# Cross-attention and a ternary feed-forward block: one pass of the attention loop put in another order on four engines

## The chip, the core and the metric

The kernel runs on one core of a Trainium2 chip. The metric is device time in microseconds (us) of one execution. Before the change it is 221.17 us, the median of 3 runs (220.5 to 221.46).

## What is computed

Eight sequences of 256 tokens with 256 features, x, attend with 16 heads of 16 to a context of 64 keys each, and pass a feed-forward block of 1024 hidden units with ternary weights and quantised activations. Scores are masked causally, so only the keys up to a token's number count.

```python
x = x + xattn(layernorm(x), ctx, Wq, Wkv_expand, Wout)     # softmax(q k^T / 4, causal) v, then Wout
h = layernorm(x)
x = x + linear_bit(silu(linear_bit(h, w1, g1)) * linear_bit(h, w2, g2), w3, g3)

def linear_bit(x, w, g):
    xq = act_quant(g * x * rsqrt(mean(x * x) + 1e-8))      # rounds x * 127 / max|x| of each token
    s = mean(|w|); wq = round(tanh(w / (s + 1e-8))) * arctanh(s)
    return xq @ wq.T
```

## The kernel before, in words

Every engine's program is written out by hand, one function per step, and the order of the calls in each engine's block is the order in which it executes. Engines wait for each other through one semaphore per kind of step (`need(engine, semaphore, value)`).

**Attention** works on one batch (one sequence, two tiles of 128 tokens) at a time. Iteration j of the loops (`def iteration(j)` on GpSimd at L398, TensorE L618, ScalarE L806, VectorE L1055) holds the second half of batch j and the first half of batch j+1. The scores of both tiles fill the PSUM tensor `wide` (4 banks); bank4 to bank7 serve everything else. In the order of one batch's data: `scores` (TensorE L511, masks first at L500), `maximum` per token and head (VectorE L907), `split_maxima` into three bf16 parts (L913, L916), `maxima_T` (TensorE L520), `maxima_T_copy` (VectorE L922), `subtract_maxima` by a matmul onto the scores (L527), `exponentials` (ScalarE L765), `half_sums` of 32 and 32 keys (GpSimd L337), `sums` with the reciprocal (VectorE L926, L929), `recip_widen` (ScalarE L751), `recip_T` (TensorE L536, through the helper at L475) and `recip_T_copy` (ScalarE L757), `probs_T` (TensorE L547, L475) and `probs_T_copy` in four pieces (L745), `weigh` (L558), `divide` (VectorE L934), `project` (L580), `residual` (VectorE L940).

Into the same iterations other work is woven: the next queries in two halves (`query`, L492, copied by ScalarE at L735), the first layer norm's statistics and power (`measure`, `aggregate`, GpSimd `norm` L327, L329), and for the feed-forward input of batch j-1 its statistics (L945, L950), GpSimd's `factor` (L343 to L348), `centre_gain` into the tile u (L958), `token_max` (L965), GpSimd's `token_scales` (L352, L356), `token_recip` (L970), `token_quant_scales` (L361), ScalarE's `quantise` (L785), `tokens_T` (L564) and its copy (L791). The weights are made ternary on the way: absolute sums (L771), means (L989), `series` and `log_input` and `log_branch` for arctanh (L994 to L1016, three elements wide), tanh (L777), `ternary` (L974).

Before the loops TensorE warms up (`keep_warm`), folds the mean into Wq (L589), and computes keys (L595), queries (L492) and values (L483) from two copies of the context that are loaded side by side into one tile (L246).

**The feed-forward loop** runs over 16 tiles T of 128 tokens: `up` in two halves (L660), `silu` (L842), `gated` (VectorE L1095), `gained` by g3 (GpSimd L425, the last tile on VectorE L1100), `square` (ScalarE L848), `scales` (GpSimd L431 to L449), `hidden_max` (VectorE L1107), `hidden_scale` (L1113, L1116), `quantise_hidden` (ScalarE L854), `hidden_T` (L671) and its copy (VectorE L1122), `down` (L684), `finish` (L1129), store. Between the loops stand the rest of batch 7's attention, and batches 5 to 7's tokens; `column_sums` (L695, copied at L1135) is needed once, before the first `down`.

In the trace a matmul of float32 shows as two passes, so that 8 rows are 4 transposes.

## Time and profile before

| What | Value |
|---|---|
| median of 3 runs | 221.17 us |
| the profiled execution, whole | 221.68 us |
| its span, first to last instruction | 219.8 us |
| mean granted TensorE clock | 0.898 of full speed |
| busy: PE, DVE, ACT, POOL | 166.9, 154.8, 143.2, 122.5 us |
| HBM traffic | 9.04 MB read, 2.10 MB written |

PE is TensorE, DVE is VectorE, ACT is ScalarE, POOL is GpSimd. The granted clock is 1.00 at 2.4 GHz and 0.50 at 1.2 GHz; a value between them in a stretch is the mean of both levels. A profile says how long each instruction was on its engine, what released an engine that had been idle, and the chain of instructions and waits that ended last. Idle time counts only where something later hangs on it.

### The profile page before, as it was taken

How to read it: one execution, taken by the hardware profiler on the slowest of the kernel's cores; microseconds unless marked ns; L12 is line 12 of the kernel's file. 1: busy time of each engine (PE TensorE's matmuls, PEld its weight loads, DVE VectorE, ACT ScalarE, POOL GpSimd, SP SyncE). 2: the span in 40 equal slices, each digit the busy share in tenths (PEclk: the TensorE clock that was granted, in tenths of full speed). 3: DMA queues.
4: the chain of work that ended last, by engine and by line, in shares of the span. 5: the costliest groups of instructions: out<-in, count | busy, mean ns of one | idle time of the engine just before them, and what ended most of it. 6: DMA issues, size and time to landing. Idle time of an engine off the chain costs nothing.

```text
span 219.8 us, 3409 instructions
## 1 busy us (share of the span) xinstructions
PE 166.9 (76%) x1114; PEld 113.1 (51%) x1114; DVE 154.8 (70%) x297; ACT 143.2 (65%) x193; POOL 122.5 (56%) x230
## 2 busy tenths in 40 slices
PE   8699679794895796696593993896666998998543
PEld 7177556563763664554562663362334464645332
DVE  0328253984689785775894896089698999999982
ACT  2033557861763865855882968658979998989740
POOL 8142807137054237238256183327789999999950
PEclk9769799999589679679999797589999999999999
DMA  7999910000000000000000000000000010100102
GB/s 145 319 378 368 374 65 0 0 4 1 0 1 0 3 0 0 0 3 0 0 1 0 3 0 0 0 3 0 0 25 25 27 48 28 48 24 24 51 24 72
DMA packets 9216, 11.35 MB, mean 52 GB/s; under 512 B 1584, under 2 KB 7984, under 8 KB 9200
## 3 DMA queue, kind: packets, MB, share of 16 engines
q1 hardware_dynamic: 8656, 10.62, 14.6%
q10 hardware_dynamic: 544, 0.52, 1.3%
q8 instruction: 9, 0.15, 0.3%
q14 instruction: 7, 0.06, 0.1%
HBM read 9.04 MB, written 2.10 MB: 51 GB/s over the span
## 4 chain that ended last, share of the span: by engine, by line
issue 21%; PE 21%; POOL 19%; DVE 18%; ACT 17%; DMA 3%; SPq 1%; POOLq 0%; DVEq 0%; ACTq 0%
ACT q_x L785 6%; PE bank L475 6%; POOL half_sum L337 5%; PE bank L492 4%; DVE row_sum L926 3%; POOL w_in L425 3%; DMA ctxT<-in_ctxT 3%; DVE u L958 2%; ACT probsT L745 2%; PE wide L511 2%; ACT wT L771 2%; PE wide L595 2%; POOL m_h L435 2%; ACT recipT L757 2%; POOL fb_a L346 2%
## 5 line engine op out<-in xcount | busy, mean ns | idle before, releaser
L425 POOL TENSOR_TENSOR w_in<-hh,g3b 128x1024 f32<-128x1024 f32 x15 | 35.4, 2360 | 1.1 <-DVE hh L1095 1.1
L660 PE MATMUL wide<-wT,xqT 128*128 128x512 bf16 x128 | 31.4, 388 | 2.2 <-DVE hh L1095 2.2
L475 PE MATMUL bank<-ident,probs 128*128 128x128 f32 x128 | 23.0, 339 | 8.6 <-ACT probsT L745 8.6
L327 POOL TENSOR_SCALAR ln_ve<-ln_mv 128x2 f32<-128x2 f32 x8 | 1.8, 227 | 46.8 <-DVE ln_mv L894 46.8
L684 PE MATMUL bank<-wT,hT 128*128 128x256 bf16 x128 | 16.7, 274 | 10.9 <-DVE hT L1122 10.0
L475 PEld LDWEIGHTS bank<-ident,probs 128*128 128x128 f32 x128 | 19.0, 176 | 11.5 <-issue 11.2
L745 ACT COPY probsT<-bank 128x512 f32<-128x512 f32 x32 | 17.6, 587 | 9.7 <-PE bank L475 9.7
L854 ACT ACTIVATE q_h<-w_in,round_c,qs_h 128x1024 f32<-128x1024 f32 x16 | 19.9, 1241 | 5.9 <-DVE qs_h L1116 5.9
L765 ACT ACTIVATE probs<-wide,ln_rstd 128x1024 f32<-128x1024 f32 x16 | 17.0, 1112 | 8.8 <-PE wide L527 8.8
L337 POOL TENSOR_TENSOR half_sum<-probs 128x512 f32<-128x512 f32 x16 | 21.9, 1389 | 0.8 <-ACT probs L765 0.8
L926 DVE TENSOR_REDUCE row_sum<-half_sum 128x32 f32<-128x1024 f32 x8 | 9.7, 1218 | 17.7 <-POOL half_sum L337 17.7
L492 PE MATMUL bank<-xT,wqT 128*128 128x256 f32 x64 | 21.7, 478 | 0.0
L684 PEld LDWEIGHTS bank<-wT,hT 128*128 128x128 f16 x128 | 11.4, 98 | 18.4 <-DVE hT L1122 16.2
L848 ACT ACTIVATE sq_junk<-hh,root_x 128x1024 bf16<-128x1024 f32 x16 | 18.3, 1144 | 2.9 <-DVE hh L1095 2.9
L1095 DVE TENSOR_TENSOR hh<-w_in,wide 128x1024 f32<-128x1024 f32 x16 | 19.3, 1209 | 0.5 <-PE wide L660 0.5
L660 PEld LDWEIGHTS wide<-wT,xqT 128*128 128x128 bf16 x128 | 11.8, 99 | 15.0 <-DVE hh L1095 2.9
L1107 DVE TENSOR_REDUCE c_max<-w_in 128x1 f32<-128x1024 f32 x16 | 19.4, 1212 | 0.0
L907 DVE TENSOR_REDUCE max_part<-wide 128x16 f32<-128x1024 f32 x16 | 18.8, 1211 | 0.5 <-PE wide L511 0.5
L842 ACT ACTIVATE w_in<-wide,dq_x 128x1024 f32<-128x1024 f32 x16 | 17.7, 1104 | 2.3 <-PE wide L660 2.3
L475 PE MATMUL bank<-ident,recip_w 128*128 128x128 f32 x32 | 6.0, 317 | 17.0 <-ACT recip_w L751 17.0
L511 PE MATMUL wide<-k_diag,qT 64*128 64x256 f32 x128 | 17.0, 403 | 0.0
L492 PEld LDWEIGHTS bank<-xT,wqT 128*128 128x128 f32 x64 | 13.7, 234 | 6.2 <-issue 4.3
(138 smaller groups left out, 360.7 us busy)
## 6 DMA issues: line engine op xcount, KB each, us to landing
out<-y SPq DMA_DIRECT2D x16, 128.0 KB, 1.7
w_in<-in_w1T SPq DMA_DIRECT2D x1, 1024.0 KB, 7.9
w_in<-in_w2T SPq DMA_DIRECT2D x1, 1024.0 KB, 11.8
w_in<-in_w3T SPq DMA_DIRECT2D x1, 1024.0 KB, 13.0
xT<-in_xT SPq DMA_DIRECT2D x1, 1024.0 KB, 9.4
x_sb<-in_x SPq DMA_DIRECT2D x1, 1024.0 KB, 11.9
x_sb<-in_x SPq DMA_DIRECT2D x2, 256.0 KB, 5.7
xT<-in_xT SPq DMA_DIRECT2D x1, 512.0 KB, 8.7
```

The costliest lines, as they stand in the source:

```text
L337: last = g.tensor_tensor(out=half_sum[:, t, :, :], in0=e[:, :, 0, :], in1=e[:, :, 1, :], op=ALU.add)
L425: g.tensor_tensor(out=c_h[:, t, :], in0=hh[:, t, :], in1=g3b[:], op=ALU.mult).then_inc(c_ready, 1)
L475: return nc.tensor.matmul(out, in_, ident[0:n, 0:n], is_transpose=True, start=True, stop=True)
L492: last = nc.tensor.matmul(bank5[:, oc * S:(oc + 1) * S], wqT[:, kc, oc * P:(oc + 1) * P], xT[:, kc, b * S:(b + 1) * S], start=(kc == 0), s ...
L511: last = nc.tensor.matmul(wide[:, n:n + PR * SK], qT[rows, c, t * P:(t + 1) * P], k_diag[rows, b % 2, c, :, :], start=(t == 1 and c == 0), ...
L660: last = nc.tensor.matmul(wide[:, (w * 2 + n) * 512:(w * 2 + n + 1) * 512], xqT[:, T, w * DC + c, :], wT[:, cols:cols + 512], start=(c == ...
L684: nc.tensor.matmul(down_banks[t][:, 0:D], hT[:, t, n, :], w_cols[:, n, :], start=(n == 0), stop=False)
L745: a.copy(probsT[:, c * PR:(c + 1) * PR, t * P:(t + 1) * P], halves[c][:].rearrange("p (n s) -> p n s", s=P)).then_inc(pT_ready, 1)
L854: a.activation(q_h[:, t, :], c_h[:, t, :], ACT.Identity, scale=qs_h[:, t:t + 1], bias=round_c[:, 2:3]).then_inc(qh_ready, 1)
L907: v.tensor_reduce(out=max_part[:, 2 * t:2 * t + 2, 0, :], in_=by_head(wide, t).rearrange("p (g n) k -> p g n k", g=2), op=ALU.max, axis=AX ...
L1095: v.tensor_tensor(hh[:, t, :], gate[:, t, :], wide[:, H:2 * H], ALU.mult).then_inc(hh_ready, 1)
L1107: v.tensor_reduce(out=c_max[:, t:t + 1], in_=c_h[:, t, :], op=ALU.max, axis=AX.X, apply_absolute_value=True).then_inc(cm_ready, 1)
```

## The change

On TensorE the maxima's transpose goes to bank5 and the transposes of the reciprocals are called behind it, behind all of the probabilities' transposes; the subtraction is called before the query's first half. ScalarE copies the reciprocals' transposes after the probabilities'. GpSimd calls `values` and `factor` before, `norm` after the half sums. VectorE takes the statistics of batch j-1 before the maxima's copy, `centre_gain` before `measure`, `ternary` before `token_max`, and the three-element weight steps after `sums`; `log_branch` moves into the middle of iteration 6. The tile u is doubled. The context comes already doubled in its layout in memory and is loaded by one transfer; four warm-up matmuls are added. An activation of one element with Exp is added behind Ln. Between the loops and in the first eight tiles of the feed-forward loop steps of batches 5 to 7 are called at other tiles.

```diff
-        u = sb("u", [P, TB, 2, D])
+        u = sb("u", [P, 2, TB, 2, D])
...
-                for n in range(2):
-                    sp.dma_start(ctxT[:, :, n, :], ctxT_d.rearrange("l (b k) -> l b k", k=SK)).then_inc(ctx_ld, 16)
+                sp.dma_start(ctxT[:].rearrange("l b n k -> l (b n k)"), ctxT_d).then_inc(ctx_ld, 16)
...
                     if live(j + 2):
                         keys(j + 2)
-                        norm(j + 2)
                     if j >= 1:
-                        factor(j - 1)
-                    if j >= 1 and live(j + 1):
...
                         values(j + 1)
-                    if live(j + 1):
-                        half_sums(j + 1)
+                        factor(j - 1)
+                    if j == B - 2:
+                        pool.wait_ge(w_down_ready, 1)
+                        product_scales(0, 4)
+                    half_sums(j + 1)
+                    if live(j + 2):
+                        norm(j + 2)
                     if j >= 1:
                         token_scales(j - 1)
...
-                pool.wait_ge(w_down_ready, 1)
-                product_scales(0, 6)
+                product_scales(4, 2)
...
-                    if T == 0:
+                    if T == 1:
                         token_scales(6)
-                    if T == 1:
+                    if T == 2:
                         token_quant_scales(6)
                         product_scales(6, 1)
-                    if T == 2:
                         factor(7)
+                    if T == 4:
                         token_scales(7)
-                    if T == 3:
+                    if T == 5:
                         token_quant_scales(7)
                         product_scales(7, 1)
...
                 def maxima_T(b):
                     need(pe, parts_ready, b + 1)
-                    need(pe, rT_ready, b)
+                    need(pe, qT_ready, b + 1)
...
-                    nc.tensor.matmul((bank4 if b else bank6)[:].bitcast(bf16)[:, 0:P], top_half(parts), ident_h[:],
+                    nc.tensor.matmul((bank5 if b else bank6)[:].bitcast(bf16)[:, 0:P], top_half(parts), ident_h[:],
...
                     need(pe, rT_ready, b + 1)
-                    if live(b + 1):
-                        need(pe, maxT_ready, b + 2)
...
                 last.then_inc(mean_done, 1)
+                keep_warm(4)
                 pe.wait_ge(wkv_ld, 16)
-                pe.wait_ge(ctx_ld, 32)
+                pe.wait_ge(ctx_ld, 16)
...
-                for oc in range(DC):
-                    query(1, oc)
+                query(1, 0)
                 pe.wait_ge(sel_ready, 1)
                 maxima_T(0)
                 pe.wait_ge(v_early, 1)
                 values_of(4)
                 subtract_maxima(0)
+                query(1, 1)
...
                 def iteration(j):
+                    scores(j + 1)
                     if j == 0:
                         pe.wait_ge(v_late, 2)
-                    if live(j + 1):
-                        scores(j + 1)
-                    if j > 0:
-                        recip_T(j)
+                    if j == 2:
+
+                        pe.wait_ge(inv_ready, 1)
                     probs_T(j, 0)
                     probs_T(j, 1)
-                    if j == 0:
-                        recip_T(j)
                     maxima_T(j + 1)
+                    recip_T(j)
+                    subtract_maxima(j + 1)
                     if live(j + 2):
                         query(j + 2, 0)
-                    subtract_maxima(j + 1)
                     weigh(j)
...
+                recip_T(7)
                 up(1, 0)
-                recip_T(7)
                 weigh(7)
-                tokens_T(5)
-                project(7)
-                column_sums()
                 for T in range(NT + 2):
                     t = T % TB
                     if live_tile(T + 1):
                         up(T + 1, 1)
+                    if T == 0:
+                        project(7)
                     if live_tile(T + 2):
                         up(T + 2, 0)
+                    if T == 1:
+                        column_sums()
...
-                    if T == 2:
-                        need(pe, xqT_ready, 6)
-                        tokens_T(6)
+                    if T == 0:
+                        need(pe, pT_ready, 4 * B)
+                        tokens_T(5)
                     if T == 4:
                         need(pe, y_ready, 2)
+                        tokens_T(6)
+                    if T == 6:
+                        need(pe, y_ready, 4)
                         tokens_T(7)
...
+                abs_sums(1)
                 act.wait_ge(half_set, 1)
 
                 def iteration(j):
-                    if j > 0:
-                        recip_widen(j)
+                    recip_widen(j)
                     if j >= 2:
                         quantise(j - 2)
-                    if j > 0:
-                        recip_T_copy(j)
                     probs_T_copy(j, 0)
-                    if j == 0:
-                        recip_widen(j)
                     probs_T_copy(j, 1)
-                    if j == 0:
-                        recip_T_copy(j)
+                    recip_T_copy(j)
                     exponentials(j + 1)
...
+                        a.activation(warm_exp[:], round_c[:, 1:2], ACT.Exp)
...
+                    if j == 6:
+                        log_branch()
                     maximum(j + 1, 0)
                     maximum(j + 1, 1)
                     split_maxima(j + 1)
...
                         measure_sum(j - 1)
+                        aggregate_sum(j - 1)
                     maxima_T_copy(j + 1)
+                    if j >= 1:
+                        centre_gain(j - 1)
                     if live(j + 2):
                         measure(j + 2)
-                    if j >= 1:
-                        aggregate_sum(j - 1)
-                        centre_gain(j - 1)
-                    if live(j + 2):
                         aggregate(j + 2)
                     divide(j)
+                    if 3 <= j < 6:
+                        ternary(j - 3)
                     if j >= 1:
                         token_max(j - 1)
-                    if 3 <= j < 6:
-                        ternary(j - 3)
+                    sums(j + 1)
                     if j == 1:
                         weight_means()
                     if j == 2:
                         series()
+                    if j == 3:
                         log_input()
-                    if j == 6:
-                        log_branch()
-                    sums(j + 1)
...
-                residual(7)
-                column_sums_copy()
                 for T in range(NT + 3):
                     t = T % TB
                     if T > 0 and live_tile(T):
                         gated(T, t)
+                    if T == 1:
+                        residual(7)
+                        measure_sum(7)
```

`log_branch` needs Ln's result from iteration 5. On the host `ctxT` is now `np.repeat(ctx[:, None], 2, axis=1)` in that layout, and SK is worked out from its doubled length.

TensorE in iteration 4, from the end of the scores (L511, in the change L512) to the projection, before:

```order
L475 MATMUL bank<-ident,recip_w 128x128 x4
L475 MATMUL bank<-ident,probs 128x128 x16
L520 MATMUL bank<-ident_h,max_part 128x128
L492 MATMUL bank<-xT,wqT 128x256 x2
L527 MATMUL wide<-neg_sel,maxT 128x512 x4
L558 MATMUL bank<-probsT,v_pair 32x256 x8
L492 MATMUL bank<-xT,wqT 128x256 x2
L564 MATMUL bank<-ident_h,q_x 128x128 x8
L580 MATMUL bank<-woutT,attnT 128x256 x4
```

TensorE at the same place in the change:

```order
L476 MATMUL bank<-ident,probs 128x128 x16
L521 MATMUL bank<-ident_h,max_part 128x128
L476 MATMUL bank<-ident,recip_w 128x128 x4
L528 MATMUL wide<-neg_sel,maxT 128x512 x4
L493 MATMUL bank<-xT,wqT 128x256 x2
L557 MATMUL bank<-probsT,v_pair 32x256 x8
L493 MATMUL bank<-xT,wqT 128x256 x2
L563 MATMUL bank<-ident_h,q_x 128x128 x8
L579 MATMUL bank<-woutT,attnT 128x256 x4
```

The reciprocals' transposes (`recip_w`) went from the head of the pass to a place behind the maxima's, and the first half of the query (`xT,wqT`) from in front of the subtraction (`neg_sel`) to behind it.

GpSimd in iteration 4, from `token_quant_scales` to the half sums, before:

```order
L361 TENSOR_TENSOR qs_x<-rm_x,fb_127a 128x4
L312 TENSOR_TENSOR k_diag<-kT,head_in 128x512
L327 TENSOR_SCALAR ln_ve<-ln_mv 128x2
L329 TENSOR_TENSOR ln_rstd<-ln_ve,neg_half 128x2
L343 TENSOR_SCALAR fb_ve<-fb_mv 128x2
L346 TENSOR_TENSOR fb_a<-fb_ve,neg_half 128x2
L348 TENSOR_SCALAR fb_127a<-fb_a 128x2
L320 TENSOR_TENSOR v_pair<-v_all,key_half 128x256
L337 TENSOR_TENSOR half_sum<-probs 128x512 x2
```

GpSimd in the change, iteration 4, from `token_quant_scales` to `norm`:

```order
L361 TENSOR_TENSOR qs_x<-rm_x,fb_127a 128x4
L312 TENSOR_TENSOR k_diag<-kT,head_in 128x512
L320 TENSOR_TENSOR v_pair<-v_all,key_half 128x256
L343 TENSOR_SCALAR fb_ve<-fb_mv 128x2
L346 TENSOR_TENSOR fb_a<-fb_ve,neg_half 128x2
L348 TENSOR_SCALAR fb_127a<-fb_a 128x2
L337 TENSOR_TENSOR half_sum<-probs 128x512 x2
L327 TENSOR_SCALAR ln_ve<-ln_mv 128x2
L329 TENSOR_TENSOR ln_rstd<-ln_ve,neg_half 128x2
```

The pair of `norm` (`ln_ve`, `ln_rstd`) now stands behind `half_sum`, and `v_pair` before `factor` (`fb_ve`, `fb_a`, `fb_127a`).

VectorE in the second half of iteration 4, from the statistics of batch 3 to the row sums, before:

```order
L945 BN_STATS fb_bn<-x_sb 128x6 x2
L922 COPY maxT<-bank 128x64
L889 BN_STATS ln_bn<-x_sb 128x6 x2
L950 BN_AGGR fb_mv<-fb_bn 128x2 x2
L958 SCALAR_TENSOR_TENSOR u<-x_sb,fb_mv,g 128x512 x2
L894 BN_AGGR ln_mv<-ln_bn 128x2 x2
L934 TENSOR_TENSOR attnT<-bank,recipT 128x512
L965 TENSOR_REDUCE u_max<-u 128x4
L974 TENSOR_SCALAR wT<-w_tanh 128x2048
L926 TENSOR_REDUCE row_sum<-half_sum 128x32
```

VectorE at the same place in the change:

```order
L943 BN_STATS fb_bn<-x_sb 128x6 x2
L948 BN_AGGR fb_mv<-fb_bn 128x2 x2
L920 COPY maxT<-bank 128x64
L956 SCALAR_TENSOR_TENSOR u<-x_sb,fb_mv,g 128x512 x2
L887 BN_STATS ln_bn<-x_sb 128x6 x2
L892 BN_AGGR ln_mv<-ln_bn 128x2 x2
L932 TENSOR_TENSOR attnT<-bank,recipT 128x512
L972 TENSOR_SCALAR wT<-w_tanh 128x2048
L963 TENSOR_REDUCE u_max<-u 128x4
L924 TENSOR_REDUCE row_sum<-half_sum 128x32
```

The statistics `fb_mv` moved ahead of `maxT`, u ahead of `ln_bn`, and the ternary weights (`wT`) ahead of `u_max`.

## Rows read from the trace of the kernel before

**Rows 1.** Stretches: us, busy time of each engine (instructions), PE's granted clock, DMA share, GB/s.
```profile
27.69:39.66 11.97, 10.69 (x81) 7.62 (x79) 6.08 (x13) 8.45 (x12) 4.42 (x5) 0.97 0.06 21
39.66:54.08 14.42, 10.47 (x83) 7.47 (x79) 10.14 (x26) 6.81 (x11) 5.45 (x10) 1.00 0.01 2
54.08:71.39 17.31, 12.92 (x83) 9.30 (x83) 14.08 (x35) 10.81 (x15) 6.72 (x12) 0.80 0.00 0
...
87.99:104.59 16.60, 12.82 (x83) 9.16 (x83) 11.25 (x25) 10.93 (x15) 7.66 (x12) 0.79 0.00 1
104.59:119.97 15.38, 10.21 (x83) 7.56 (x83) 10.93 (x24) 10.24 (x16) 7.36 (x12) 1.00 0.00 1
119.97:133.02 13.05, 10.57 (x73) 7.55 (x73) 11.75 (x25) 10.70 (x15) 6.52 (x12) 0.87 0.01 1
...
137.12:174.13 37.01, 27.81 (x191) 15.85 (x190) 27.04 (x45) 29.61 (x42) 25.79 (x51) 0.90 0.04 12
174.13:205.00 30.87, 28.01 (x206) 16.43 (x203) 29.10 (x48) 28.45 (x35) 29.44 (x49) 1.00 0.11 35
```

**Rows 2.** The chain that ended last, pass 5: start, length, engine, tile and line.
```profile
105.15 2.08 ACT q_x L785 x4
...
113.58 1.40 POOL fb_a L346
...
115.89 2.45 POOL half_sum L337 x2
118.36 1.23 DVE row_sum L926
...
119.62 0.36 DVE recip L929
```

**Rows 3.** The timeline of pass 5: start, length, engine, line, operation, out<-in.
```profile
105.35 0.63 PE L475 MATMUL bank<-ident,recip_w 128*128 128x128 f32 x4 [2.64 <-ACT recip_w L751]
...
108.32 1.07 PE L475 MATMUL bank<-ident,probs 128*128 128x128 f32 x8 [1.47 <-ACT probsT L745]
...
109.28 1.08 PE L492 MATMUL bank<-xT,wqT 128*128 128x256 f32 x4
...
110.29 0.39 PE L527 MATMUL wide<-neg_sel,maxT 32*128 32x512 bf16 x4
...
110.74 2.12 ACT L765 ACTIVATE probs<-wide,ln_rstd 128x1024 f32<-128x1024 f32 x2 [0.68 <-PE wide L527]
...
112.61 1.21 DVE L965 TENSOR_REDUCE u_max<-u 128x4 f32<-128x1024 f32 x1
...
113.73 1.22 DVE L974 TENSOR_SCALAR wT<-w_tanh 128x2048 bf16<-128x2048 f32 x1
```

**Rows 4.** The timeline where VectorE and GpSimd meet, passes 2, 3 and 6.
```profile
65.65 1.20 DVE L995 TENSOR_SCALAR w_tmp<-w_tmp 128x3 f32<-128x3 f32 x1
...
82.35 1.65 DVE L974 TENSOR_SCALAR wT<-w_tanh 128x2048 bf16<-128x2048 f32 x1
82.88 3.48 POOL L337 TENSOR_TENSOR half_sum<-probs 128x512 f32<-128x512 f32 x2
...
130.76 0.16 DVE L1012 TENSOR_TENSOR w_tmp<-w_tmp 128x3 f32<-128x3 f32 x1
```

**Rows 5.** ScalarE's timeline in pass 6.
```profile
125.55 1.28 ACT L765 ACT_TABLE_LOAD   x1
126.84 2.12 ACT L765 ACTIVATE probs<-wide,ln_rstd 128x1024 f32<-128x1024 f32 x2
```

**Rows 6.** The start: TensorE's timeline, a stretch of it, the context's loads (us to landing).
```profile
7.75 3.65 PE L595 MATMUL wide<-ctxT,wkvT 64*128 64x512 f32 x4 [2.05 <-DMA ctxT<-in_ctxT]
11.32 3.63 PE L492 MATMUL bank<-xT,wqT 128*128 128x256 f32 x8
...
7.90:14.60 6.70, 6.70 (x12) 3.40 (x11) 2.36 (x7) 0.59 (x1) 2.87 (x4) 0.50 1.06 379
...
ctxT<-in_ctxT SPq DMA_DIRECT2D x2, 128.0 KB, 5.5
```

54 lines of the change are left out of this document (27 added, 27 removed).

## Prediction

> **What bounds the kernel now.** I read the page first (shares of busy time, no engine above 76%), then the stretches of the attention loop and of the feed-forward loop, then the chain of waits through one pass, then the timeline of that pass. Call R(j) the moment at which VectorE has batch j's reciprocals (L929 ends), and pass j what lies between R(j) and R(j+1).
>
> The stretches [rows 1] are passes 0 to 6 (pass 3 is as long as pass 4 and left out), the turn from attention to feed-forward (from GpSimd's first product with g3, L425, to its seventh), and the steady tiles after it. Passes 1 to 6 take 13.05 to 17.31 us while no engine is busy for more than 14.08 of it: a chain bounds them. The steady tiles take 30.87/8 = 3.86 us, with GpSimd at 29.44 of 30.87; the change does not touch what they do. The turn holds six tiles in 37.01 us, where six steady ones would take 23.2.
>
> The chain of pass 5 [rows 2] shows the links that matter: ScalarE's quantise, then, after transposes and exponentials, GpSimd's factor standing **before** its half sums, which start at 115.89 although the first exponentials began at 110.74 [rows 3]; then row_sum and recip. The same pass in order of time [rows 3] shows TensorE putting a query half (109.28) between the maxima's transpose and the subtraction at 110.29. So two things are late: the subtraction, behind a query half, and the half sums, behind GpSimd's small work.
>
> **The change, part by part.** Times are in us after R(j) unless said otherwise; R(5) of before is 104.59.
>
> *A pass with TensorE at 2.4 GHz.* ScalarE's quantise ends at 2.6 as before (105.15 + 2.08 [rows 2]). With no reciprocals' copy in between, the first two probability copies end at 3.65. TensorE's second half of transposes takes 1.07 behind the first of them and ends near 4.4, the maxima's transpose at 4.5; the reciprocals' transposes (0.63) come behind it, half of that beside the maxima's copy on VectorE; the subtraction (0.39) runs 5.15 to 5.55, and the exponentials start at 5.8, behind the copy of the reciprocals [rows 3]. Before it was 110.74 - 104.59 = 6.15. The larger gain is behind it: with norm moved back and factor done by about 6, the half sums start 1.25 after the exponentials (half of their 2.12, and a hand-over) and take 2.45 [rows 2]: 7.05 to 9.5, where they ended at 13.7. Row sum and reciprocal (1.23 + 0.36) would make a pass of 11.1.
>
> *What is late next is VectorE.* Behind the maxima's copy (4.8) it has u, the next layer norm, and then divide, which needs TensorE's subtraction, one query half (1.08) and the weighing: divide ends at 8.5, u_max (1.21 [rows 3]) at 9.75, row_sum starts there: 11.35. In passes 1 and 2 the scores come 0.35 to 0.7 late, since project and scores now follow each other with less to spare: 11.7 and 12.05. Before 14.42 + 17.31 [rows 1]: **-8.0**.
>
> *Passes 3 to 5 hold a ternary step.* It comes right behind divide, at 8.5, in the middle of the second half sum. That pair has a price [rows 4]: when VectorE's weight step came first (82.35), the half sums took 3.48 instead of 2.45; when the half sum came first, a three-element step waited for it and took 1.20 instead of 0.16. So ternary starts at 9.55, takes 1.22 [rows 3] to 10.8, u_max ends at 12.0, the pass is 13.65. The bounds are 12.75 (the half sum is the one that waits; it has a microsecond of cover from u_max) and 14.7 (both wait); I take the middle since by these times the half sum has started. The Trainium skill, "SBUF — State Buffer", section "Who interferes with whom", says that VectorE and GpSimd share one pair of ports as an exclusive lock, and that whoever issues first blocks the other for its whole instruction. Both rows agree with it; without a lock the total would be 2.7 lower.
>
> The weight steps moved behind the sums now delay the head of the next pass: series (8 steps of some 0.2 with their waits [rows 4]) lands in pass 3, log_input (4 steps) in pass 4. Quantise waits for a reciprocal and a product behind them, so pass 3 becomes 15.1 and pass 4 14.2. Sum 15.1 + 14.2 + 13.7 = 43.0 against 16.60 + 16.60 + 15.38 = 48.58 [rows 1]: **-5.6**.
>
> *Pass 6.* No ternary and no query. log_branch (6 steps, 1.3) delays the maxima, product_scales (three short steps, 0.9) delays the half sums: 12.8 against 13.05: **-0.2**. The table of Exp was loaded for 1.28 right before the exponentials [rows 5]; warm_exp puts that load behind Ln at the end of pass 5, where ScalarE finishes 0.8 after R(6): counted in the 12.8. The Trainium skill, "ScalarE: Activation LUTs", section "What ACT_TABLE_LOAD costs", adds a drain of 1.38 to each such load. In rows 5 the load starts at 125.55 with no idle ahead of it and the next activation starts at 126.84, so no drain shows; with two drains pass 6 would be 2.8 longer, and the total 202.8.
>
> *The start.* TensorE waits 2.05 for the second context load, its granted clock is 0.50 from 7.90 to 14.60, and the keys (3.65) and first queries (3.63) run at that level [rows 6]. The two loads took 5.5 each; one load with long rows, issued where the first was, lands by about 6.9 (SP issues all loads behind it one issue, 0.6, earlier, and none of those is waited for here), and the four warm-up matmuls (eight passes like those that take 1.07 in rows 3) fill TensorE from 5.70 to 6.75. Keys then run from 6.8 at half their time, and queries end at 10.6, 4.3 earlier. Of this 1.7 is given back, since the second query half, its copy and a values copy now stand ahead of the first exponentials. R(0) comes at 25.05 instead of 27.69: **-2.6**. Bounds: +0.7 if the clock falls all the same, -4.3 if nothing is given back.
>
> *Pass 0.* It has no quantise; the maxima's transpose no longer shares a bank with the reciprocals, so it doesn't wait for their copy: R(1) comes at 9.6 instead of 11.97 [rows 1]: **-2.4**.
>
> *The turn.* project(7), tokens and column sums are pushed behind the up matmuls, GpSimd's product scales are split, token steps are spread over six tiles. From R(7) = 133.02 to the first gained tile at 137.12 [rows 1] it was 4.1; it becomes 3.3. Then, tile by tile: gained 1 to 6 follow after 6.5, 6.6, 7.1, 4.0, 4.3 and 5.1 = 33.6, because the first hidden scale still waits behind residual(7), its statistics and the copy of the column sums, and tile 2 carries token scales, product scales and factor(7) on GpSimd. ScalarE takes two quantises (2.08 each) and two token copies with only 30.87 - 28.45 = 2.4 of slack in eight tiles, and ends up 1.3 later behind. Sum -0.8 - 3.4 + 1.3: **-2.9**. Bounds: 0 and -8, as the order of four engines here is the least certain.
>
> **The sum**: -2.6 - 2.4 - 8.0 - 5.6 - 0.2 - 2.9 = -21.7. The profiled execution took 221.68 (span 219.8, 1.9 around it), 0.5 above the median of the runs shown, 221.17. 221.7 - 21.7 = **200.0**.
>
> **The rivals.** *The clock at the start falls anyway and TensorE is slow in part of each pass.* In pass 4 it is granted 0.79 on average [rows 1], with long waits for the reciprocals. In the new order its longest wait, for ScalarE's first copy, is about 1 us, which speaks against. Price: 3.3 at the start, and for transposes (1.07), reciprocals (0.63) and subtraction (0.39) at half clock half of the time in six passes about 4.4: 207.7.
>
> *VectorE and GpSimd collide more than counted.* u (two inputs in SBUF) meets factor, and the weight steps meet norm. 0.8 more in each of seven passes: 205.6. For it: rows 4. Against it: u has 0.9 of slack before divide.
>
> *No lock, and a turn with less waiting.* 200.0 - 2.7 - 3: 194.3.
>
> *TensorE stays at the low clock through the loop, and it is slower than before.* Pass 5 of before has 10.21 of TensorE work at a clock of 1.00 [rows 1]; at 1.2 GHz that is 20.4, which would bound six passes instead of 15.6 on average: +29, less the 8 gained elsewhere: 243. It decides from a pass of 17.0 on. Against it: a pass with 10.2 us of work in 13 us has shorter waits than the 15.38 of that pass, which was granted 1.00 throughout.
>
> *The change moves nothing much:* the half sums stay late because factor in front of them waits for batch j-1's statistics. These are now taken before the maxima's copy, so VectorE would have to be two microseconds late: about 215.
>
> **How the numbers follow.** The forecast of 200.0 has 0.60; 194.3 has 0.10; 205.6 and 207.7 together 0.20; the drains 0.04; 215 0.03; 243 0.03. The range, 194 to 207.5, leaves out 243, 215, half of 207.7 and a little of the fast end. A measurement of this kernel can tell about 0.5% from no change. All cases but 243 are faster, with 0.01 kept for a turn that eats the gain: faster 0.96, same 0.01, slower 0.03.
>
> **What would show it.** Right: half_sum starting about 1.3 us after the exponentials in every pass; passes of 11.5 to 12 (1, 2) and 13 to 15 (3 to 5); keys at about 1.9 us in all; TensorE granted over 0.9 in the loop; steady tiles still at 3.86. Wrong: exponentials more than 7 us after the reciprocals, row_sum waiting for GpSimd, or a turn over 37 us.

## The result and the profile after

The change makes the kernel faster: 196.29 us median (194.60 to 199.26, 4 runs) against 220.83 (219.79 to 221.46) beside it, ratio 0.887 with a 95% interval of 0.879 to 0.894. The forecast was 200.0 with a range of 194 to 207.5: right in sign and range, 3.7 us too slow. The profiled execution of the changed kernel took 194.60 (span 192.9), so profile against profile 26.9 us of span are gone, by medians 24.5. One execution each of two experiments was disturbed (377 and 300 us), and the ratios are of the undisturbed and fastest executions of both kernels, so that a ratio can differ from that of two medians.

The stretches of the changed kernel, cut at its own R(0) to R(7), then the turn, then five steady tiles; columns as in [rows 1]:

```profile
25.20:34.74 9.54, 9.21 (x71) 6.46 (x69) 5.98 (x14) 7.74 (x11) 4.06 (x5) 0.99 0.26 90
34.74:45.45 10.71, 10.19 (x81) 7.44 (x79) 9.93 (x22) 5.94 (x10) 6.78 (x11) 1.00 0.01 3
45.45:56.56 11.11, 9.81 (x81) 7.11 (x79) 10.41 (x26) 9.70 (x15) 7.13 (x12) 1.00 0.00 1
56.56:70.87 14.31, 12.40 (x105) 9.17 (x102) 13.48 (x32) 11.73 (x16) 8.00 (x12) 1.00 0.01 1
70.87:83.28 12.41, 9.31 (x78) 6.90 (x78) 11.73 (x28) 10.71 (x15) 8.19 (x12) 1.00 0.00 1
83.28:96.14 12.86, 11.32 (x95) 8.20 (x92) 12.32 (x25) 11.63 (x18) 7.99 (x12) 1.00 0.01 2
96.14:109.27 13.13, 9.93 (x61) 6.34 (x60) 10.20 (x25) 9.73 (x15) 7.11 (x15) 0.74 0.00 0
112.78:145.49 32.71, 25.32 (x173) 13.87 (x172) 27.25 (x45) 28.40 (x41) 26.79 (x51) 0.94 0.04 14
157.56:176.81 19.25, 17.91 (x129) 10.33 (x127) 18.90 (x31) 17.98 (x23) 18.35 (x31) 1.00 0.10 35
```

The seven passes take 84.07 us where they took 105.33 (27.69 to 133.02 in [rows 1]); in passes 1 to 5 VectorE is now busy for all but 0.5 to 0.8 us. The steady tiles stand at 19.25 / 5 = 3.85, as before.

Pass 5 of the changed kernel in order of time, to be laid beside [rows 2] and [rows 3]:

```profile
88.03 0.39 PE L528 MATMUL wide<-neg_sel,maxT 32*128 32x512 bf16 x4
88.63 2.14 ACT L766 ACTIVATE probs<-wide,ln_rstd 128x1024 f32<-128x1024 f32 x2
89.92 2.50 POOL L337 TENSOR_TENSOR half_sum<-probs 128x512 f32<-128x512 f32 x2 [0.45 <-ACT probs L766]
90.55 0.69 DVE L932 TENSOR_TENSOR attnT<-bank,recipT 128x512 f32<-128x512 f32 x1 [0.37 <-PE bank L557]
91.16 2.34 DVE L972 TENSOR_SCALAR wT<-w_tanh 128x2048 bf16<-128x2048 f32 x1
93.42 1.21 DVE L963 TENSOR_REDUCE u_max<-u 128x4 f32<-128x1024 f32 x1
94.55 1.20 DVE L924 TENSOR_REDUCE row_sum<-half_sum 128x32 f32<-128x1024 f32 x1
```

The half sums start 1.29 after the exponentials; they started 5.15 after them [rows 2, 3]. The row sum no longer waits for GpSimd but for VectorE's own row: the ternary (wT), standing against the second half sum, takes 2.34 instead of 1.22, and the maxima follow it. So VectorE is what ends the pass, as the prediction said; in passes 2 to 5 it ends the pass or comes level with the half sums, in pass 1 the row sum waits 0.31 for GpSimd. In pass 4 the same two met the other way round: the ternary came first and kept its 1.22, the half sums took 3.58, and the pass is 12.41:

```profile
78.06 3.58 POOL L337 TENSOR_TENSOR half_sum<-probs 128x512 f32<-128x512 f32 x2 [0.45 <-ACT probs L766]
79.30 1.22 DVE L972 TENSOR_SCALAR wT<-w_tanh 128x2048 bf16<-128x2048 f32 x1
```

In pass 6 the row sum waits 1.03 us for GpSimd. Its half sums stand behind factor and behind the product scales, which the change itself put there, and start 2.49 after the exponentials (102.66):

```profile
105.15 2.48 POOL L337 TENSOR_TENSOR half_sum<-probs 128x512 f32<-128x512 f32 x2
107.67 1.22 DVE L924 TENSOR_REDUCE row_sum<-half_sum 128x32 f32<-128x1024 f32 x1 [1.03 <-POOL half_sum L337]
```

The start, TensorE's timeline and the load, answers to [rows 6]: the keys start 0.6 earlier, and keys and queries run at 2.4 GHz (granted 1.00 from 7.16 to 11.04).

```profile
5.65 1.05 PE L480 MATMUL wide<-ones 128*128 128x128 f32 x8
7.16 1.95 PE L595 MATMUL wide<-ctxT,wkvT 64*128 64x512 f32 x4 [0.46 <-DMA ctxT<-in_ctxT]
9.04 2.00 PE L493 MATMUL bank<-xT,wqT 128*128 128x256 f32 x8
```

ScalarE's tables at the end of pass 5, beside [rows 5]:

```profile
93.20 1.28 ACT L826 ACT_TABLE_LOAD   x1
94.49 0.20 ACT L826 ACTIVATE w_ln<-w_ln 128x3 f32<-128x3 f32 x1
94.72 1.28 ACT L828 ACT_TABLE_LOAD   x1
96.01 0.20 ACT L828 ACTIVATE warm_exp<-round_c 128x1 f32<-128x1 f32 x1
```

Between loads and activations lies nothing longer than 0.03 us: here too the trace shows no drain, against the rule that the prediction quotes from the Trainium skill, "ScalarE: Activation LUTs", section "What ACT_TABLE_LOAD costs".

### The profile page after: what moved, and what is told of

Same layout as the page of the kernel before. It is cut to its first block, busy times and chain, and to the rows that moved or that the text cites. A ratio compares the mean times of both kernels' runs of the same rounds, so it can differ in the third digit from the quotient of the medians.

```text
span 192.9 us, 3424 instructions
## 1 busy us (share of the span) xinstructions
PE 159.0 (82%) x1122; PEld 107.7 (56%) x1122; DVE 154.0 (80%) x297; ACT 143.2 (74%) x194; POOL 127.7 (66%) x233
## 3 DMA queue, kind: packets, MB, share of 16 engines
HBM read 9.04 MB, written 2.10 MB: 58 GB/s over the span
## 4 chain that ended last, share of the span: by engine, by line
DVE 29%; PE 27%; POOL 14%; ACT 13%; issue 12%; DMA 3%; SPq 0%; DVEq 0%; POOLq 0%; ACTq 0%
POOL half_sum L337 6%; DVE hh L1093 5%; DVE c_max L1105 5%; ACT q_x L786 5%; PE bank L476 4%; DVE row_sum L924 4%; PE wide L657 4%; PE bank L493 3%; ACT probsT L746 3%; POOL w_in L426 3%; DMA ctxT<-in_ctxT 3%; ACT probs L766 3%; PE bank L557 3%; PE wide L512 3%; PE bank L579 2%
## 5 line engine op out<-in xcount | busy, mean ns | idle before, releaser
L657 PE MATMUL wide<-wT,xqT 128*128 128x512 bf16 x128 | 33.5, 405 | 0.8 <-DVE hh L1093 0.8
L337 POOL TENSOR_TENSOR half_sum<-probs 128x512 f32<-128x512 f32 x16 | 21.1, 1338 | 10.1 <-ACT probs L766 10.0
L476 PE MATMUL bank<-ident,probs 128*128 128x128 f32 x128 | 17.2, 278 | 11.6 <-ACT probsT L746 11.6
L681 PE MATMUL bank<-wT,hT 128*128 128x256 bf16 x128 | 17.6, 283 | 9.0 <-DVE hT L1120 9.0
L476 PEld LDWEIGHTS bank<-ident,probs 128*128 128x128 f32 x128 | 13.8, 141 | 15.8 <-issue 15.6
L746 ACT COPY probsT<-bank 128x512 f32<-128x512 f32 x32 | 17.0, 584 | 4.5 <-PE bank L476 4.5
L493 PE MATMUL bank<-xT,wqT 128*128 128x256 f32 x64 | 17.8, 404 | 0.0
L786 ACT ACTIVATE q_x<-u,round_c,qs_x 128x256 f32<-128x256 f32 x32 | 16.6, 591 | 1.6 <-POOL qs_x L361 1.6
L512 PE MATMUL wide<-k_diag,qT 64*128 64x256 f32 x128 | 17.0, 404 | 0.0
L579 PE MATMUL bank<-woutT,attnT 128*128 128x256 f32 x64 | 16.6, 404 | 0.0
L343 POOL TENSOR_SCALAR fb_ve<-fb_mv 128x2 f32<-128x2 f32 x8 | 2.6, 331 | 19.3 <-DVE fb_mv L948 19.3
```

The source lines that it names most:

```text
L337: last = g.tensor_tensor(out=half_sum[:, t, :, :], in0=e[:, :, 0, :], in1=e[:, :, 1, :], op=ALU.add)
L476: return nc.tensor.matmul(out, in_, ident[0:n, 0:n], is_transpose=True, start=True, stop=True)
L493: last = nc.tensor.matmul(bank5[:, oc * S:(oc + 1) * S], wqT[:, kc, oc * P:(oc + 1) * P], xT[:, kc, b * S:(b + 1) * S], start=(kc == 0), s ...
L512: last = nc.tensor.matmul(wide[:, n:n + PR * SK], qT[rows, c, t * P:(t + 1) * P], k_diag[rows, b % 2, c, :, :], start=(t == 1 and c == 0), ...
L657: last = nc.tensor.matmul(wide[:, (w * 2 + n) * 512:(w * 2 + n + 1) * 512], xqT[:, T, w * DC + c, :], wT[:, cols:cols + 512], start=(c == ...
L681: nc.tensor.matmul(down_banks[t][:, 0:D], hT[:, t, n, :], w_cols[:, n, :], start=(n == 0), stop=False)
```

## The experiments

### GpSimd's order alone, TensorE's order alone

The kernel before with one side of the change each. GpSimd's:

```diff
                     if live(j + 2):
                         keys(j + 2)
-                        norm(j + 2)
                     if j >= 1:
-                        factor(j - 1)
...
                         values(j + 1)
-                    if live(j + 1):
-                        half_sums(j + 1)
+                        factor(j - 1)
+                    half_sums(j + 1)
+                    if live(j + 2):
+                        norm(j + 2)
```

> The kernel before with GpSimd's order alone: values and factor before, norm behind the half sums. Theory: the half sums' late start was the largest part of each pass, so they now start about 1.3 us after factor or the exponentials, whichever is later (factor still waits for statistics that VectorE takes behind the maxima's copy, about 5.7 after the reciprocals), and a pass falls by 2.5 to 3.5 us in passes 2 to 5 until VectorE's u_max or ternary ends last: 205 to 211 us. Rival (the gain comes from TensorE's order, the half sums only follow it): under 4 us of gain, 217 us or more.

TensorE's (with the copies that follow it on ScalarE and the maxima's other bank):

```diff
-                    if j > 0:
-                        recip_T(j)
                     probs_T(j, 0)
                     probs_T(j, 1)
                     maxima_T(j + 1)
+                    recip_T(j)
+                    subtract_maxima(j + 1)
                     if live(j + 2):
                         query(j + 2, 0)
-                    subtract_maxima(j + 1)
```

> The kernel before with the order of TensorE and ScalarE alone: maxima's transpose in bank5, reciprocals' transposes behind it, subtraction before the query half. Theory: the exponentials start 0.3 to 1.3 us earlier in each pass, but the half sums still wait for norm and factor, whose statistics don't depend on them, so most is lost: 1 to 6 us of gain, 215 to 220 us. Rival (TensorE's order is the main part): 12 us or more of gain, 209 us or less.

Measured: GpSimd's order alone 208.26 us, the median of 205.96, 205.98, 210.54 and 377, ratio 0.944 (0.915 to 0.973); its seven passes take 91.36. TensorE's alone 218.44 with before at 220.46 beside it, ratio 1.010 (1.000 to 1.020), so no gain that its times show; passes 102.98. So GpSimd's side carries 14.0 of the 21.3 us that the passes lost and TensorE's alone 2.35. The changed kernel has 4.9 more than their sum; VectorE's new order is in that too, and no run has it alone or leaves it out. Part of the 14.0 is TensorE's clock: GpSimd's order alone was granted 1.00 in passes 1 to 6. In passes 1 and 5, where before had 1.00 as well, it gains 2.3 and 2.0; in passes 2 to 4, where before had 0.79 to 0.80 [rows 1], 3.0 to 3.3. Pass 3 of the kernel with GpSimd's order alone shows what then holds it (timeline): the exponentials come 6.1 after R(3), as in [rows 3], the half sums only 2.08 behind them, since factor still waits for statistics, and, 3.50 long beside the ternary, they hold the row sum.

```profile
70.34 2.12 ACT L764 ACTIVATE probs<-wide,ln_rstd 128x1024 f32<-128x1024 f32 x2 [0.68 <-PE wide L526]
72.42 3.50 POOL L337 TENSOR_TENSOR half_sum<-probs 128x512 f32<-128x512 f32 x2
75.95 1.22 DVE L925 TENSOR_REDUCE row_sum<-half_sum 128x32 f32<-128x1024 f32 x1 [1.17 <-POOL half_sum L337]
```

With TensorE's order alone the half sums still begin 4.25 behind the exponentials (78.63 and 74.38 in its pass 3), so little of an earlier subtraction reaches the row sum.

### Norm back in front of the half sums

```diff
                         keys(j + 2)
+                        norm(j + 2)
...
                     half_sums(j + 1)
-                    if live(j + 2):
-                        norm(j + 2)
```

> The changed kernel with norm put back in front of factor and the half sums on GpSimd, nothing else. Theory: norm waits for the next layer norm's statistics, which VectorE now takes behind u at about 7 us after the reciprocals, so factor and the half sums end 2 to 3 us later than they do (12 instead of 9.5 after the reciprocals) and become the last thing in passes 1, 2 and 6; passes 3 to 5 lose less, as the ternary step then runs first: 6 to 15 us lost, 202 to 211 us. Rival (VectorE alone bounds the passes, the half sums have cover): under 3 us lost, 199 us or less.

Measured: 211.63 us (210.52 to 212.45), ratio 0.970 (0.955 to 0.984), passes 101.68: this one edit gives back 17.6 of the 21.3 us, all of it in passes 1 to 5 (3.1 to 4.2 each; the theory had passes 3 to 5 losing less, and pass 6, which has no norm, losing too). TensorE's clock, 0.78 to 0.89 in passes 2 to 5 where the changed kernel has 1.00, is in that number. GpSimd stands 5.1 to 7.4 us for the layer norm's statistics in passes 0 to 5; its timeline in pass 4 (R at 81.57) shows 6.40, with factor and the half sums behind it:

```profile
90.03 0.22 POOL L327 TENSOR_SCALAR ln_ve<-ln_mv 128x2 f32<-128x2 f32 x1 [6.40 <-DVE ln_mv L891]
90.34 0.71 POOL L329 TENSOR_TENSOR ln_rstd<-ln_ve,neg_half 128x2 f32<-128x2 f32 x1
91.71 0.19 POOL L343 TENSOR_SCALAR fb_ve<-fb_mv 128x2 f32<-128x2 f32 x1
93.92 2.50 POOL L337 TENSOR_TENSOR half_sum<-probs 128x512 f32<-128x512 f32 x2
```

It is the wait that matters and not the work behind it: norm's two operations are 0.93 us, its wait 6.40.

### The query half back in front of the subtraction

```diff
                     recip_T(j)
-                    subtract_maxima(j + 1)
                     if live(j + 2):
+                        need(pe, maxT_ready, j + 2)
                         query(j + 2, 0)
+                    subtract_maxima(j + 1)
```

> The changed kernel with the first query half put back in front of the subtraction (it waits for the maxima's copy, as both use bank5). Theory: the exponentials and half sums come about 1.1 us later, the weighing and divide at the same time as now; VectorE's u_max gives them cover of 0 to 0.3 in passes 1 and 2 and of more in passes 3 to 5: 2 to 5 us lost, 198 to 201 us. Rival (the place of the subtraction is what makes the passes short): 8 us or more lost, 204 us or more.

Measured: 200.64 us median (198.18 to 205.65), ratio 0.916 (0.894 to 0.938). The profiled execution is the 205.65, in which TensorE is granted 0.79 to 0.88 in passes 2 to 6, so only the median gives a price: 4.3 us, within what the theory said but uncertain by some 2.

### The start: either half alone

The changed kernel without `keep_warm(4)`; and, apart, with it but with two loads of the old layout:

```diff
-                sp.dma_start(ctxT[:].rearrange("l b n k -> l (b n k)"), ctxT_d).then_inc(ctx_ld, 16)
+                for n in range(2):
+                    sp.dma_start(ctxT[:, :, n, :], ctxT_d.rearrange("l (b k) -> l b k", k=SK)).then_inc(ctx_ld, 16)
```

> The changed kernel without the four extra products that TensorE makes on ones between its first block of 28 and the keys (they compute nothing that is kept). Theory: they bridge the wait for the context, so without them TensorE waits some 1.3 us more in front of the keys, its granted clock falls to about 0.5 there, keys take about 3.65 and queries 3.63 instead of 1.95 and 2.00, and the end of the first reciprocals comes 2.5 to 3.5 us later than 25.2, with nothing won back behind: about 199 us, ratio 0.897 to 0.912 by the changed kernel's 0.8867. Rival: the wait is too short to matter, keys and queries stay at 1.95 to 2.0, reciprocals at 25.2, and the time stays at 196.3.

> The changed kernel with the context loaded by two transfers of one copy each, as before, instead of one transfer of a doubled layout; all else as changed. Theory: the second transfer lands some 0.3 to 1.0 us later than the single one, keys start at 7.5 to 8.1 instead of 7.16, still at full clock since the four extra products lie in front of them; first reciprocals at 25.5 to 26.2, time 196.5 to 197.3, that is of the 2.5 us at the start the layout carries under 1 and the clock the rest. Rival: the longer wait lets the clock fall after all, keys and queries at about 3.65, first reciprocals at 28 or later, time 199 or more.

Measured: 197.47 us (196.54 to 198.68) without the extra products, 196.34 (193.29 to 199.34) with two loads. The theory on the extra products was wrong; TensorE's timeline without them:

```profile
6.96 1.95 PE L594 MATMUL wide<-ctxT,wkvT 64*128 64x512 f32 x4 [0.48 <-DMA ctxT<-in_ctxT]
8.84 1.99 PE L493 MATMUL bank<-xT,wqT 128*128 128x256 f32 x8
```

Laid side by side, the starts of six profiles give the price of each part:

| kernel | wait, then keys start | keys | queries | R(0) | R(0) less keys' start |
|---|---|---|---|---|---|
| before [rows 6] | 2.05, 7.75 | 3.65 | 3.63 | 27.69 | 19.94 |
| TensorE's order alone | 1.43, 7.36 | 2.52 | 3.78 | 27.27 | 19.91 |
| GpSimd's order alone | 1.10, 7.50 | 1.95 | 3.65 | 25.76 | 18.26 |
| changed, two loads | 0, 7.69 | 1.95 | 1.99 | 25.74 | 18.05 |
| changed, no extra products | 0.48, 6.96 | 1.95 | 1.99 | 25.01 | 18.05 |
| changed | 0.46, 7.16 | 1.95 | 2.00 | 25.20 | 18.04 |

The last column goes with how long the clock is down, and not with which products it catches: with GpSimd's order alone TensorE is granted 0.50 from 9.60 to 13.00, and R(0) comes 0.2 later behind the keys' start than in the changed kernel; with TensorE's order alone it is 0.50 from 8.60 to 15.30, and before from 7.90 to 14.60 [rows 6], and R(0) comes 1.9 later in both, though the keys take 2.52 in one and 3.65 in the other. The changed order of calls at the start, which only the last three rows have, is in these differences and was not run alone. In the one profile of each, either edit by itself keeps the clock: one with a short wait, the other by filling it. How much of the earlier start of the keys comes from the layout is uncertain: over all profiles they start at 7.36 to 7.75 with two loads and at 6.65 to 7.55 with one.

### The old order between the loops

The changed kernel with before's order on four engines behind the last reciprocals (GpSimd's product scales stay split as in the change); its core:

```diff
-                recip_T(7)
                 up(1, 0)
+                recip_T(7)
                 weigh(7)
+                tokens_T(5)
+                project(7)
+                column_sums()
...
                 centre_gain(6)
...
+                residual(7)
```

> The changed kernel with the order between the two loops (TensorE, ScalarE, VectorE, GpSimd behind the last reciprocals) as it was before. Theory: the turn from the last reciprocals to GpSimd's tenth gained product, 48.3 us in the changed kernel and 52.7 before, goes back to 51 to 53 while the seven passes stay at 84 us in sum: 199 to 201 us. Rival: the turn's gain came from arriving earlier or from the clock, and not from its order: the stretch stays at 48 to 49 and the time at 196 to 197.

Measured: 196.50 us (195.97 to 198.76), the changed kernel's time. From R(7) to GpSimd's tenth gained product it takes 49.92, where the changed kernel takes 48.29 and the kernel before 52.67: neither the theory's 51 to 53 nor the rival's 48 to 49. Two things beside the order are in these numbers. The first is when ScalarE comes to the last reciprocals. It widens them 1.23 after R(7) before, and 0.03 after R(7) with the old order in the changed kernel (R(7) is 133.02 and 109.13):

```profile
134.25 0.61 ACT L751 COPY recip_w<-recip 128x512 f32<-128x512 f32 x1
```
```profile
109.16 0.62 ACT L748 COPY recip_w<-recip 128x512 f32<-128x512 f32 x1 [0.88 <-DVE recip L922]
```

In the changed kernel's own profile it is 1.06, behind up products that came late in a pass 6 with TensorE at 0.74. Four other profiles of the changed order have 0.03 as well (its second profile, no extra products, two loads, the query half back in front). To the seventh gained product they take 35.18 to 35.21, and the old order takes 38.35. So with ScalarE equally early the order is worth 3.1 us in the profiles, and nothing that the medians show.

The second is TensorE's clock. The first two stretches from R(7) on, before and then with the old order in the changed kernel,

```profile
133.02:137.12 4.10, 1.63 (x8) 1.66 (x9) 2.71 (x7) 3.31 (x6) 1.30 (x4) 0.64 0.00 0
137.12:149.30 12.18, 10.52 (x59) 5.96 (x58) 5.64 (x8) 6.97 (x12) 3.77 (x8) 0.70 0.01 1
```
```profile
109.13:113.17 4.04, 2.37 (x16) 1.71 (x16) 2.64 (x7) 3.02 (x6) 1.30 (x5) 1.00 0.00 0
113.17:123.23 10.06, 7.70 (x48) 5.04 (x50) 5.71 (x8) 5.95 (x10) 3.79 (x7) 0.83 0.01 2
```

hold nearly the same work; in the second TensorE is granted 1.00 and 0.83 instead of 0.64 and 0.70, and it is 2.2 us shorter. The kernel with TensorE's order alone stands between them: before's order, ScalarE at 1.22 much as before, TensorE granted 0.85 in the second stretch, and 11.16 us for it where before has 12.18 and the old order in the changed kernel 10.06. So about 1.0 goes with the clock and 1.1 with ScalarE. A full clock in the pass before doesn't help by itself: the kernel with GpSimd's order alone has 1.00 in pass 6, then 0.70 and 0.69, and takes 52.90 to the tenth product.

### The ternary behind the maxima

```diff
-                    if 3 <= j < 6:
-                        ternary(j - 3)
                     if j >= 1:
                         token_max(j - 1)
+                    if 3 <= j < 6:
+                        ternary(j - 3)
```

> The changed kernel with one edit on VectorE: in passes 3 to 5 the ternary step (wT, 1.22 alone, 2.34 beside a half sum) goes behind the reduction to the maxima instead of in front of it. Theory: the ternary's 1.1 us of standing against a half sum is gone in the passes where the two meet (3 and 5), and the maxima, 1.21 us earlier, let TensorE transpose them earlier; row sums start when the second half sum ends. Passes 3 to 5 go from 39.6 to 36.5 to 38.5 us, time 193.5 to 195.5 us. Rival: the maxima now meet the half sum instead, or the row sums wait for GpSimd's second half sum in any case, so that the order on VectorE changes nothing: passes at 39 to 40.5, time 196 to 197.

Measured: 195.11 us (194.35 to 195.38), the time that the theory gave; but passes 3 to 5 take 39.2, which is the rival's figure and hardly less than the changed kernel's 39.6. It was then run beside the changed kernel itself:

> The changed kernel as it is, beside the next two on one chip. The theory of its spread: in passes 3 to 5 the ternary step and GpSimd's second half sum come to the read of the same memory within a few hundredths of a microsecond, and in each pass either may go first; where the ternary loses it takes 2.2 to 2.4 us instead of 1.22 and the next reciprocals are 1.1 us later, so the runs lie within 3 x 1.1 us and what TensorE's clock adds: 194 to 199.5, median about 196.3. Rival: the spread is the clock's alone, and then the kernel with the ternary moved spreads as widely.

> The ternary step behind the maxima in passes 3 to 5, as before on another chip, now beside the changed kernel itself. Theory: 0.5 to 2 us under the changed kernel's median here, and all runs within 1.5 us of each other, since no ternary meets a half sum. Rival: the same median and the same spread as the changed kernel.

Measured: the changed kernel 195.10 us (190.99 to 199.41, 6 runs), the ternary last 193.08 (190.44 to 196.37), with before at 220.05. The timeline of its first profile shows the collision gone in pass 5:

```profile
90.25 2.51 POOL L337 TENSOR_TENSOR half_sum<-probs 128x512 f32<-128x512 f32 x2 [1.25 <-ACT probs L766]
91.49 1.21 DVE L963 TENSOR_REDUCE u_max<-u 128x4 f32<-128x1024 f32 x1
92.62 1.23 DVE L972 TENSOR_SCALAR wT<-w_tanh 128x2048 bf16<-128x2048 f32 x1
93.77 1.20 DVE L924 TENSOR_REDUCE row_sum<-half_sum 128x32 f32<-128x1024 f32 x1
```

The reduction to the maxima beside a half sum keeps its 1.21, and the ternary comes when the half sums end. But the theory of the spread fell: this kernel spreads over 6 us as well. In this comparison its runs are of two kinds by TensorE's mean clock: 190.44, 190.63 and 191.11 at 0.981, and 195.04 to 196.37 at 0.938 to 0.948. The one run of the changed kernel at 0.981 took 190.99. At 0.981 the two kernels don't differ, and between 0.938 and 0.950 the changed kernel took 193.89 to 199.41, so the mean clock alone doesn't order the runs. Whether moving the ternary gains anything isn't settled; a collision costs 1.1 us in its pass.

### The quantise behind the exponentials

On ScalarE, with the ternary last:

```diff
                     recip_widen(j)
-                    if j >= 2:
-                        quantise(j - 2)
                     probs_T_copy(j, 0)
                     probs_T_copy(j, 1)
                     recip_T_copy(j)
                     exponentials(j + 1)
+                    if j >= 2:
+                        quantise(j - 2)
```

> The ternary behind the maxima, and on ScalarE the quantise of the batch two back (four activations, 2.08 us) behind the exponentials instead of between the reciprocals' widening and the copies of the transposed exponentials. In the changed kernel TensorE waits 1.99 us for these copies in passes 2 to 6, and in some passes its clock then falls, so that eight transposes take 1.94 instead of 1.06. Theory: the copies 2 us earlier bring exponentials to 3.9 to 4.3 us after the reciprocals instead of 5.3 to 7.3, the wait and the fall of the clock go, and passes 3 to 6 shorten until VectorE or ScalarE, each busy 11 to 12 us in them, fills them: passes 3 to 5 go from 39.2 us to 35.5 to 37.5, pass 6 from 12.65 to 11.5 to 12.5, in all 2 to 5 us, time 190 to 193.5. Rival: the tokens' transposes and the projection then wait for the quantise, and VectorE's own order fills the pass anyway: passes 3 to 5 at 38.5 to 39.5, time 194.5 to 195.5.

Measured: 196.32 us (194.28 to 197.40), ratio 0.893 (0.885 to 0.901): nothing gained on the kernel with the ternary last beside it, whose runs at the same mean clock (0.938 to 0.948) took 195.04 to 196.37; none of the six came at 0.981. Passes 3 to 5 did shorten, to 13.25, 12.37 and 11.90 (37.5 in sum). Pass 6 stayed at 13.16: earlier exponentials don't help where the half sums stand behind factor and the product scales, and the row sum waits 2.35 for them. From R(7) to the tenth gained product it took 50.56 instead of 48.29. In pass 6, without a query half between, TensorE now waits for the quantise itself, and its clock falls behind that wait, so that the output's products take 3.60 where pass 6 of the second run of the ternary last had 1.99 (timeline):

```profile
103.55 0.40 PE L563 MATMUL bank<-ident_h,q_x 128*128 128x128 bf16 x4 [2.08 <-ACT q_x L786]
104.76 3.60 PE L579 MATMUL bank<-woutT,attnT 128*128 128x256 f32 x8
105.69 1.22 DVE L924 TENSOR_REDUCE row_sum<-half_sum 128x32 f32<-128x1024 f32 x1 [2.35 <-POOL half_sum L337]
```

ScalarE then widens the last reciprocals 3.02 after R(7) instead of 0.62. In pass 6 the wait has only changed its place.

### TensorE's waits filled

With the ternary last, products on ones (their result is thrown away) in the long waits:

```diff
                     probs_T(j, 0)
+                    if j >= 2:
+                        need(pe, qT_ready, j + 2)
+                        need(pe, maxT_ready, j + 1)
+                        fill(bank5, 8 if j == 2 else 12)
                     probs_T(j, 1)
...
                 def hidden_T(T, t):
-                    need(pe, qh_ready, T + 1)
                     need(pe, hT_ready, T - 1)
+                    if T in (0, 5):
...
+                        fill(hT_banks[t], 14)
+                    need(pe, qh_ready, T + 1)
```

> The kernel with the ternary behind the maxima, with extra products on ones (nothing of them is kept) in the places where TensorE waits longest for ScalarE: in passes 2 to 6 between the two halves of the exponentials' transposes (8 in pass 2, 12 in the others, 1.05 to 1.6 us in waits of 1.3 to 2.5), and 14 (1.85 us) ahead of the transposes of the first and of the sixth hidden tile (waits of 2.1 and 2.45). Theory: in the runs so far TensorE's granted clock falls to 0.5 for some 3 us behind these waits, in some passes of one run and not of the next, and that is most of the spread between 190.4 and 199.4 us; the fastest runs have a mean clock of 0.981 and lie at 190.4 to 191.1. With the waits filled the mean clock is 0.97 to 0.99 in every run and the time 189.5 to 191.5 in each, spread under 2 us. Rival: the clock falls for another reason, at the same places or at others: mean clock 0.94 to 0.95, time 193 to 196 and as spread as before.

Measured: 198.29 us (195.79 to 198.45), ratio 0.904 (0.896 to 0.912), mean clock 0.956 to 0.982. The mechanism came out and the price did not. Through the loop and most of the turn TensorE is granted 1.00 (stretch, columns as in [rows 1]); filled, none of these waits is followed by a fall.

```profile
27.00:144.00 117.00, 108.22 (x865) 80.57 (x869) 100.46 (x209) 96.65 (x140) 76.96 (x131) 1.00 0.02 6
```

But I had counted a product as 0.13 us; each is two matmuls in the trace, and twelve took 2.84, longer than the waits that they fill (1.85 to 2.46 in the two profiles without them). In the loop that cost nothing that shows: its passes take 84.21, against 83.31 and 85.29 in those two. The last fill stands a tile too late: TensorE waits 2.54 ahead of it, its clock falls behind that wait, and the fill then delays the next tile, which takes 7.57 instead of 4.14 and 4.45 (timeline).

```profile
72.24 2.84 PE L484 MATMUL bank<-ones 128*128 128x128 f32 x24
144.59 0.61 PE L567 MATMUL bank<-ident_h,q_h 128*128 128x128 bf16 x8 [2.54 <-ACT q_h L863]
149.42 3.29 PE L484 MATMUL bank<-ones 128*128 128x128 f32 x28
```

Half as many products, and the last fill a tile earlier, were not tried. That the held clock saves time in the loop is therefore not shown by this kernel; behind the last gained product the profiles do show what the clock costs (below).

## Why the prediction was right, and where its terms were off

Term by term, profile against profile, measured behind the forecast:

| term | forecast | measured |
|---|---|---|
| start, to R(0) | -2.6 | -2.49 |
| pass 0 | -2.4 | -2.43 |
| passes 1 and 2 | -8.0 | -9.91 |
| passes 3 to 5 | -5.6 | -9.00 |
| pass 6 | -0.2 | +0.08 |
| turn, R(7) to the tenth gained product | -2.9 | -4.38 |
| behind it | 0 | +1.23 |
| sum | -21.7 | -26.9 |

**The chain and its next bound: right.** Half sums 1.3 after the exponentials in passes 2 to 5 (1.67 in pass 1, 2.5 in pass 6), and then VectorE's divide, maxima and row sum as the end of passes 2 to 5; in pass 6 the row sum waits 1.03 for GpSimd, which the prediction had named as a sign of being wrong. That norm in front of the half sums was what held them is shown by putting it back (17.6 us). That each side alone gains less than the change is shown by running it; what VectorE's order adds is argued only.

**Passes 1 and 2: mis-sized by 1.9.** The step was "scores come 0.35 to 0.7 late". They did not: pass 2 is 11.11, just the 11.1 of the plain schedule, with exponentials at 5.68 after R (forecast 5.8), half sums 6.97 to 9.47 (7.05 to 9.5), divide to 8.29 (8.5) and maxima to 9.42 (9.75). And pass 1 has no quantise, which I had left in: exponentials at 4.90, pass 10.71.

**Passes 3 to 5: mis-sized by 3.4.** Ternary waiting for the second half sum was "the middle" at 13.65. The profile has it in passes 3 and 5 (2.35 and 2.34), with the price named, and the other order in pass 4, where I had given 12.75 as the bound: 12.41. In pass 5, where the order was the forecast one, VectorE's divide also ended 7.96 after R instead of 8.5. Over five profiles with the ternary in its changed place the three passes take 39.0 to 43.3 us (39.6, 41.9, 43.3, 43.2, 39.0), so the forecast of 43.0 is a possible outcome and the high end. Two things differ between them: who comes first (1.1 us a pass) and, not in my sum at all, whether TensorE's eight transposes behind its wait for the copies run in 1.06 or 1.94 and what follows them too (exponentials at 5.35 after R(5) in one profile, 6.67 in another). The rule of the Trainium skill, "SBUF — State Buffer", section "Who interferes with whom", held here in both orders: who had come first kept its time, the other paid 1.1. Where the ternary comes in the middle of the first half sum, both pay: 2.01 and 3.50 in pass 4 of the kernel with the query half back in front.

**The rival of the clock** was priced at 4.4 in the loop, against "its longest wait is about 1 us". That reason failed: TensorE waits 1.30 to 3.10 for ScalarE's copies in passes 2 to 6, since the quantise stands ahead of them. The fall came in some passes only: in pass 6 in the first profile, in passes 4 and 6 in the second, whose pass 4 has its exponentials at 7.22 after R instead of 5.90 and takes 14.71 instead of 12.41 (about 1.0 of that is the collision).

**Pass 6: right in size**, with no drain; TensorE was granted 0.74 in it, which the forecast did not have, and exponentials came at 6.52. The exponentials didn't set its length: in seven profiles with the changed order the half sums start 9.01 to 9.04 after R(6), with exponentials anywhere from 6.24 to 6.72, since factor and the product scales come first. That the product scales delay them was in the forecast.

**The turn: right in sign, too small by 1.5, and the order is not all of it.** I put it all down to the order. With ScalarE equally early the order is worth 3.1 (above). Two terms were not in my sum, as they come with the loop: ScalarE comes earlier to the last reciprocals (1.1), and TensorE is granted more in the first two stretches (1.0); some 0.6 between the third and the fourth gained product stays open. Against them the changed kernel's profile loses 1.0 by its own late pass 6 and 0.5 between the seventh and the tenth product. The tiles themselves came as 5.33, 5.97, 7.14, 4.02, 4.34 and 5.91 (forecast 6.5, 6.6, 7.1, 4.0, 4.3, 5.1).

**The end: a term put at nothing.** The 1.23 lie behind GpSimd's last gained product, whose work the change leaves as it was. Stretches from there to the end (columns as in [rows 1]), before, changed, and the changed kernel without the extra products:

```profile
205.00:219.80 14.80, 5.96 (x60) 4.79 (x60) 10.10 (x18) 4.96 (x5) 6.45 (x14) 0.99 0.13 44
```
```profile
176.81:192.90 16.09, 7.32 (x60) 5.59 (x60) 10.38 (x20) 5.13 (x7) 6.52 (x14) 0.89 0.13 42
```
```profile
178.67:196.90 18.23, 9.62 (x60) 6.78 (x60) 10.20 (x18) 4.96 (x5) 6.43 (x14) 0.64 0.11 37
```

The same 60 matmuls take 5.96, 7.32 and 9.62 as the granted clock goes from 0.99 to 0.89 and 0.64, and the stretch grows with them. In all fourteen profiles its length follows the clock, from 14.77 at 0.99 to 18.27 at 0.64; TensorE's order alone, with before's end, has 15.96 at 0.88. So this end alone differs by up to 2.3 us between the profiles of the changed kernel and its variants. Why the clock falls there in some and not in others stays open.

**The start: right in sum, not in its parts.** I gave the extra products the clock; the shorter wait alone keeps it, and so do the products alone. Queries end 3.91 earlier (forecast 4.3), and 1.42 of that is given back up to R(0) (forecast 1.7).
